# A two-stage graph network on one core: chunk residues in one row on VectorE, a residual moved on GpSimd, and the attention mask added by GpSimd instead of TensorE

## The reference

```python
h = relu(layernorm(x)); x = x + L0(h, adj)
h = relu(layernorm(x)); x = x + L1(h, adj)
# L0: scores = leaky_relu(f1[:, :, None] + f2[:, None, :], 0.2), -1e9 where adj == 0,
#     elu(softmax(scores) @ h)
# L1, for each of 3 layers l:
#     scores = leaky_relu(si[:, :, None] + sj[:, None, :] + attn_b[l], 0.2)
#     scores = where(adj + eye > 0, scores, -inf)
#     h = layernorm(x + softmax(scores) @ x, g1[l], beta1[l])
#     x = layernorm(h + gelu(h @ W1[l] + b1[l]) @ W2[l] + b2[l], g2[l], beta2[l])
```

## Time and profile before

| | |
|---|---|
| median of 3 runs | 2756.68 us (2756.49 to 2758.12) |
| profiled execution, its own time | 2756.0 us |
| its span, first to last instruction | 2754.2 us |
| TensorE clock granted, mean | 0.987 of full speed |
| busy: TensorE, VectorE, ScalarE, GpSimd | 96%, 78%, 80%, 61% |
| TensorE waits for a g_low before second / before hidden | 15.2 us in 29 waits / 5.6 us in 8 |

### The profile page before, as it was taken

How to read it: one execution, slowest core, us unless ns; L and a number is a source line. 1 busy time by engine, 2 the same in 40 slices (tenths; PEclk the granted TensorE clock), 3 DMA queues, 4 the chain that set the end, 5 groups by cost and what they waited for, 6 DMA issues and landing times.

```text
span 2754.2 us, 53331 instructions
## 1 busy us (share of the span) xinstructions
PE 2652.4 (96%) x16771; PEld 2388.7 (87%) x16868; DVE 2139.7 (78%) x7999; ACT 2201.9 (80%) x4494; POOL 1677.8 (61%) x2181
## 2 busy tenths in 40 slices
PE   4699999999999999999999999999999999999997
PEld 3688988898889898988898989898888898998997
DVE  6998787877787877787877888877888767677674
ACT  4889888888888888888887888888888777777774
POOL 4466666557676556566666566555676554454555
PEclk7899999999999999999999999999999999999999
DMA  6222222222122212122322121212132211111121
GB/s 203 75 73 85 70 94 73 77 74 94 63 93 66 77 64 74 51 76 81 100 74 88 45 81 66 78 56 89 60 104 81 68 36 52 42 46 53 50 64 54
DMA packets 118590, 203.43 MB, mean 74 GB/s; under 512 B 12801, under 2 KB 85537, under 8 KB 118305
## 3 DMA queue, kind: packets, MB, share of 16 engines
q1 hardware_dynamic: 118304, 199.97, 22.5%
HBM read 116.05 MB, written 83.89 MB: 73 GB/s over the span
## 4 chain that ended last, share of the span: by engine, by line
PE 72%; DVE 12%; POOL 8%; issue 5%; ACT 2%; DMA 1%; SPq 0%; DVEq 0%; POOLq 0%; ACTq 0%
PE bank L605 33%; PE bank L588 27%; PE ps_u L564 7%; POOL xo L374 3%; DVE g_lo L988 3%; DVE st L962 2%; POOL rs L1295 2%; PE ps_u L646 2%; PE ps_s L559 2%; DVE ub L1081 2%; PE ps_s L551 1%; POOL hb L374 1%; DVE ub L957 1%; ACT g_hi L862 1%; ACT bank L864 1%
## 5 line engine op out<-in xcount | busy, mean ns | idle before, releaser
L605 PE MATMUL bank<-w_hi,g_hi 128*128 128x256 f32 x3072 | 890.9, 290 | 15.4 <-DVE g_lo L988 15.2
L605 PE MATMUL bank<-w_hi,g_lo 128*128 128x256 f32 x3072 | 865.8, 282 | 0.0
L605 PE MATMUL bank<-w_lo,g_hi 128*128 128x256 f32 x3072 | 864.4, 281 | 0.0
L862 ACT ACTIVATE g_hi<-bank,b_eff 128x512 fp32r<-128x512 f32 x768 | 529.7, 690 | 334.2 <-PE bank L588 327.9
L988 DVE TENSOR_TENSOR g_lo<-bank,g_hi 128x512 fp32r<-128x512 f32 x768 | 519.5, 687 | 201.5 <-ACT bank L864 186.2
L588 PE MATMUL bank<-zt_hi,w_hi 128*128 128x512 f32 x1536 | 632.6, 412 | 9.3 <-DVE g_lo L988 5.6
L588 PE MATMUL bank<-zt_hi,w_lo 128*128 128x512 f32 x1536 | 607.4, 395 | 0.0
L588 PE MATMUL bank<-zt_lo,w_hi 128*128 128x512 f32 x1536 | 606.3, 395 | 0.0
L605 PEld LDWEIGHTS bank<-w_hi,g_hi 128*128 128x128 f32 x3072 | 579.5, 189 | 24.1 <-DVE g_lo L988 22.9
L605 PEld LDWEIGHTS bank<-w_lo,g_hi 128*128 128x128 f32 x3072 | 579.8, 189 | 0.8
L605 PEld LDWEIGHTS bank<-w_hi,g_lo 128*128 128x128 f32 x3072 | 579.2, 189 | 0.0
(11 more groups left out here) (96 smaller groups left out, 4141.1 us busy)
## 6 DMA issues: line engine op xcount, KB each, us to landing
xb<-x_scratch SPq DMA_DIRECT2D x88, 512.0 KB, 4.0
x_scratch<-xo SPq DMA_DIRECT2D x64, 512.0 KB, 4.8
xin<-in_x SPq DMA_DIRECT2D x38, 512.0 KB, 4.7
r_scratch<-elu_r SPq DMA_DIRECT2D x32, 512.0 KB, 3.0
xin<-r_scratch SPq DMA_DIRECT2D x32, 512.0 KB, 4.7
out<-xo SPq DMA_DIRECT2D x32, 512.0 KB, 3.6
m<-m_scratch SPq DMA_DIRECT2D x96, 128.0 KB, 3.7
x_scratch<-h SPq DMA_DIRECT2D x24, 512.0 KB, 2.9
```

Of the source, the lines that this page charges most:

```text
L605: mm = pe.matmul(y, g[:, c, r * P:(r + 1) * P], w[:, l, c, :], start=(c == 0 and n == 0), stop=(c == C - 1 and n == 2))
L862: act.activation(g_hi[:, c, :], block_in, ACT.Gelu, bias=bias).then_inc(g_hi_ready, 1)
```

## The change

Four edits. VectorE: `g_low(4)` to `g_low(7)` stand in one row, `second_statistics` behind them, with a small copy ahead of `second_variance`; in middle steps `first_lows` comes behind the first half of `next_dots`. GpSimd: `residual` of a unit moves from the end of step s+1 behind `first_root` of step s+2. ScalarE: in middle steps `second_norm` comes ahead of `first_exps`. And from step 5 on the mask is no longer added by TensorE in PSUM: GpSimd adds it to the relu tile that ScalarE makes (`e1` of unit s+2 at the start of step s, `e0` in middle steps), and `row_lows` waits for that (`masked_ready`) where it waited for `above_ready`. `spare` grows from 8 to 72 columns and its slices move.

```diff
+        def aside(u):
+            return u - 2 >= ASIDE
+        def aside0(v):
+            return early_step(v) + 1 >= ASIDE
...
                     if live(s + 1):
-                        sp.wait_ge(scores_ready, st.nth(s + 1))
+                        if aside(s + 1):
+                            sp.wait_ge(masked_ready, st.nth(s + 1 - 2 - ASIDE))
+                        else:
+                            sp.wait_ge(scores_ready, st.nth(s + 1))
...
-                pe.matmul(scores[:, :], ident_b[:, :], mask.rearrange("p t m -> p (t m)"),
-                          start=False, stop=True, skip_group_check=True).then_inc(done, 1)
+                if mask is not None:
+                    mm = pe.matmul(scores[:, :], ident_b[:, :], mask.rearrange("p t m -> p (t m)"),
+                                   start=False, stop=True, skip_group_check=True)
+                mm.then_inc(done, 1)
...
                 next_exps()
+                if only_middle(s) and not first_chunk:
+                    second_norm()
                 first_exps()
...
                 def next_lows():
                     if live(s + 2):
+                        taken = spare[:, 4 + T:5 + T]
+                        if aside(s + 2):
+                            row_lows(st.nth(s - ASIDE), taken, e1, ps_s, low, masked_ready, low_ready)
+                        else:
+                            row_lows(st.nth(s + 2), taken, e1, ps_s, low, above_ready, low_ready)
...
                 g_low(4)
                 g_low(5)
+                g_low(6)
+                g_low(7)
                 second_statistics()
-                g_low(6)
+                dve.tensor_copy(spare[:, 4:4 + T], neg_half[:, :])
                 second_variance()
-                g_low(7)
                 input_variance()
...
+                next_dots(range(T // 2))
                 if only_middle(s):
                     first_lows()
-                next_dots(range(T // 2))
...
+                def next_masked():
+                    if live(s + 2) and aside(s + 2):
+                        pool.wait_ge(above_ready, st.nth(s + 2))
+                        pool.wait_ge(m_in, 16 * st.nth(s + 2))
+                        take_waits(2)
+                        pool.tensor_tensor(e1[:, :, :], e1[:, :, :], m1[s % 2][:, :, :], ALU.add).then_inc(masked_ready, 1)
...
+                next_masked()
                 first_root()
                 if v3 is not None and v3 < CH:
                     made_root()
+                if live(s - 2) and s - 2 < U - 1:
+                    residual(pool, st, s - 2)
                 scaled_rows()
...
+                if only_middle(s):
+                    first_masked()
                 if v3 is not None and v3 >= CH:
                     made_root()
...
                     affine(pool, st, s - 1)
-                    residual(pool, st, s - 1)
```

More of the change, by code:

```diff
@@ L65, in build @@
     LATE = 4
+    ASIDE = 5
     U = L * G
@@ L225, in build @@
         above_ready = sem("above_ready")
+        masked_ready = sem("masked_ready")
         low_ready = sem("low_ready")
@@ L324, in early_norm @@
             return s == -1
+        def aside(u):
+            return u - 2 >= ASIDE
+        def aside0(v):
+            return early_step(v) + 1 >= ASIDE
+        ASIDE0 = min(v for v in range(G) if aside0(v))
         def x_rows(v):
@@ L884, in body @@
                     return
-                second_norm()
+                if not only_middle(s):
+                    second_norm()
                 make_rows()
@@ L1344, in made_root, with first_masked @@
                         inverse_root(st.nth0, v3, ve3, rs3, ve3_ready, rs3_ready)
+                def next_masked():
[4 more added lines that the diff above has]
+                        pool.tensor_tensor(e1[:, :, :], e1[:, :, :], m1[s % 2][:, :, :], ALU.add).then_inc(masked_ready, 1)
+                def first_masked():
+                    if v1 is not None and aside0(v1):
+                        pool.wait_ge(above0_ready, st.nth0(v1))
+                        pool.wait_ge(masks0_ready, st.nth0(v1))
+                        take_waits(3)
+                        pool.tensor_tensor(e0[:, :, :], e0[:, :, :], m0[:, :, :], ALU.add).then_inc(masked0_ready, 1)
                 def mask():
```

40 lines of the change are left out of this document (25 added, 15 removed).

## The result

The changed kernel takes 2784.61 us (median; 2784.34 to 2785.99) where the kernel before takes 2756.59: 1.0103 of its time (95% interval 1.009 to 1.0117), 28 us slower. The forecast was 2761.3 us, with a range of 2736 to 2778.

What follows compares the result with a forecast made beforehand. TensorE, busy 96%, was taken to bound the kernel: matmuls plus stops. Terms +29.9 - 20.8 - 3.0 - 5.1 - 4.4 + 2 + 6 = +4.6 us on 2756.0, median 0.7 above, gave 2761.3 us; range 2736 to 2778.

Steps and rivals of the forecast that it cites:

- middle steps 15 to 72: Twenty middle steps go from 546.1 to 576 us, as late VectorE work and GpSimd's mask add delay `hidden(7)`: +29.9 us.
- entering steps 14 to 71: Twenty entering steps lose the stop at g_low(7) and the mask's matmul, each falling to 26.03 us: -20.8 us.
- The residual: On GpSimd ahead of `scaled_rows`, it delays entering steps of layer 2 by 0.4 us in five steps: +2 us.
- steps 5, 8, 11: Early entering steps gain from the row of low halves and the mask's missing matmul: -3.0 us.
- late steps 7 to 73: In 23 late steps TensorE is not stopped and saves the mask's matmul of 0.22 us each: -5.1 us.
- steps 74 to 93: Twenty steps in which TensorE saves the mask's matmul of 0.22 us each: -4.4 us.
- steps 6, 9, 12: Early middle steps, already late from weight preparation, lose 1.9 us more each: +6 us.
- The row's part: In middle steps VectorE's `vb` starts 3.68 us in, not 2.00; without the add's wait the step takes 27.55 us.
- The add's part: GpSimd's mask add, taken as 1.35 us behind `affine`, makes row minima to g_low(3) 1.25 us later in middle steps.
- the two moves that were priced at nothing: ScalarE's `second_norm` ahead of `first_exps`, VectorE's `first_lows` behind half the dots, in middle steps: no cost, VectorE having over 0.5 us.
- The add is long: Rival: GpSimd's mask add takes 1.95 us, each middle step 0.6 us longer, +14 us, 2775 us; chance 0.20.
- The two faster cases: Rivals: add off the path, middle steps 27.55, 2732 us, chance 0.15; no lateness either, 26.44, 2705 us, chance 0.10.

Runs made afterwards that it cites:

- res_only: The kernel before with only the residual moved behind `first_root`, as the change moves it; 2766.17 us, ratio 1.0035.
- res_back: The changed kernel with the residual back behind `affine` at the end of GpSimd's step; 2800.72 us, ratio 1.016.
- g3_first: The changed kernel with g_low(3) ahead of `first_norm` in steps from 14 on that carry a residual; 2764.21 us, ratio 1.0022.
- row_only: The kernel before with only g_low(4) to g_low(7) in one row and the short copy ahead of `second_variance`; 2771.04 us, ratio 1.0054.
- mask_only: The kernel before with only the mask added by GpSimd to the relu tile from step 5 on; 2778.86 us, ratio 1.008.
- no_mid_add: The changed kernel with unit s+2's mask in middle steps up to 72 added by TensorE again; 2772.65 us, ratio 1.0055.
- no_swaps: The changed kernel with `second_norm` and the first dots of middle steps back in their old order; 2783.51 us, ratio 1.0098.
- part_only: The kernel before with g_low(6) ahead of `second_statistics`, g_low(7) inside it, and the short copy, in entering steps from 14 on; 2756.41 us, ratio 0.9999.

## Why the prediction was wrong

The direction was right, the size not: +28 us against +4.6. Term by term, from the steps of the two traces:

| term of the sum | forecast | measured |
|---|---|---|
| middle steps 15 to 72 | +29.9 | +32.5 |
| entering steps 14 to 71, with "The residual" | -20.8 + 2 | -14.7 |
| steps 5, 8, 11 | -3.0 | +0.9 |
| late steps 7 to 73 | -5.1 | +1.0 |
| steps 74 to 93 | -4.4 | +0.3 (to 95) |
| steps 6, 9, 12 | +6 | +6.1 |
| behind TensorE's last matmul | 0 | +2.4 |

**The step that failed is "The residual."** It was priced as later `scaled_rows` in five entering steps, "with VectorE's small instructions held on the way I take 0.4 us in five steps: +2", and nothing in late, plain and middle steps. What stood beside it was not a small instruction but `first_norm`, in every step that carries a residual: the group of 380 such instructions goes from 407 ns each to 506, in res_only to 507, in res_back back to 408. The rows with which it could have been seen were there: the earlier trace rows shows L973 held by just these four instructions, and `first_norm` waits for the very root behind which they were put. The prediction asked of L973 what a GpSimd instruction beside it does, and did not ask it of `first_norm`.

Against the forecast, in rounded means, this is 9 x 0.55 = 5.0 us in late steps, 6 x 0.8 = 4.8 in the last six and 3.7 in entering ones. In middle steps with a residual it is 9 x (29.63 - 28.8) = 7.5 more: the forecast had taken them to be as long as those without, and they are 1.3 longer. Together this is 21 us, and g3_first, which takes away only this way, is 20 us faster than the change. The move as such was no mistake beside the row and the mask, where it gains 16 us; its price was what the forecast had wrong.

**The middle steps** came out at 28.93 on the mean, against 28.8, but that is luck in part: those with a residual are 0.8 longer than forecast, those without 0.45 shorter. The row's part was right: `vb` at 3.59 (forecast 3.68), `affine`'s end at 9.26 (9.35), and 27.68 us with the row alone in row_only, where the sum without the add gives 28.8 - 1.25 = 27.55. The add's part was too large, 1.25 against 0.66. The add takes 1.17 us, not 1.35; the prediction's own rule, two instructions of 0.70 less a start-up of 0.20, gives 1.20, so the 1.35 does not follow from it. It also starts 9.34 into the step, not 9.60, so it ends at 10.53 and not 10.95, and `hidden(7)` starts 14.15 in, where 14.67 was forecast. That the row alone already lengthens the middle step, and the add only on top of it, is what the sum said, and row_only, mask_only and no_mid_add show it.

**The entering and late steps without a residual** (26.05, forecast 26.03; 28.22, forecast 28.21) and the plain ones were right. Late step 7 is an exception: it takes 29.10 us, and 28.22 in no_swaps, so there the two moves that were priced at nothing cost 0.9.

**Steps 5, 8 and 11** lose where they should gain: row_only has them at 26.26 us, mask_only at 28.42 (27.03 before), so it is the mask's add, for which the prediction had no price there. GpSimd in step 8, which begins at 340.42 in the kernel before and at 340.43 in mask_only, is busy with weight preparation and then `affine` until 8.8 us into the step in both. Then comes `first_root` in the one and the add in the other, so the root starts 1.3 us later:

```profile
349.18 1.02 POOL L1295 TENSOR_TENSOR rs<-ve,neg_half 128x4 f32<-128x4 f32 x1
```

```profile
349.34 1.18 POOL L1379 TENSOR_TENSOR e<-e,m 128x512 f32<-128x512 f32 x1
350.46 1.03 POOL L1323 TENSOR_TENSOR rs<-ve,neg_half 128x4 f32<-128x4 f32 x1
```

**The end** had no term in the sum: the program ends 15.1 us behind TensorE's last matmul before and 17.5 after. It is the row's doing, since row_only ends 17.6 behind and mask_only and res_only 15.1. In the last steps the row had no stop to take away, but it puts the statistics of unit 94 behind g_low(7) and all that follows them 2.2 us later. The last unit's root (the last row here) then finds GpSimd still at the unit before:

```profile
2761.08 2.83 POOL L387 TENSOR_TENSOR xo<-xo,g_row 128x256 f32<-128x256 f32 x4 [2.39 <-ACT xo L759]
2763.99 2.78 POOL L387 TENSOR_TENSOR xo<-xo,beta_row 128x256 f32<-128x256 f32 x4
2766.85 2.76 POOL L387 TENSOR_TENSOR xo<-xo,xin 128x256 f32<-128x256 f32 x4
2769.57 1.02 POOL L1327 TENSOR_TENSOR rs<-ve,neg_half 128x4 f32<-128x4 f32 x1
```

In part_only, which changes entering steps alone, the same root waits for its own variance only, and the span ends 2.4 us nearer to TensorE's last matmul:

```profile
2741.38 1.02 POOL L1338 TENSOR_TENSOR rs<-ve,neg_half 128x4 f32<-128x4 f32 x1 [0.64 <-DVE ve L997]
```

None of the rivals was this one. "The add is long" gave the nearest time (2775) for a reason that did not occur. The two faster cases needed middle steps of 27.55 us or less; they are 28.35 and 29.63.

## What to carry to other kernels

Work that is moved to just behind an instruction runs beside whatever else that instruction releases: before moving it, list who waits for the same semaphore on the other engines, and whether the two may run at the same time. An engine with a fixed order gains nothing from an earlier start of one piece if a wait in front of the next is thereby exposed; price a move in the step behind as well, and in the last steps of the program. And apply each part only in the kinds of step where the trace shows room: the change's edits cost 28 us when made everywhere; the useful ones, placed by kind of step and with two reorderings beside them, gave 30.

## What the runs showed of the hardware

VectorE's `first_norm` (tensor_scalar, 128x256, fp32, SBUF to SBUF) beside GpSimd instructions of the same size: its four instructions take 1.38 us alone, 1.62 beside four one-input instructions of 0.43, 2.74 beside four two-input ones of 0.75, and in these two cases the last ends 0.14 to 0.16 us behind GpSimd's last. GpSimd is hardly slowed (2.98 for four two-input ones, 2.81 alone). The Trainium skill, SBUF — State Buffer, section "Who interferes with whom", says that a tensor_scalar can enter a 2-port mode and that whoever issues first then gets the shared port pair for the whole instruction. The traces agree that GpSimd instructions of this size hold it, one-input ones too (1.62 us in place of 1.38); in which mode `first_norm` runs, no run here shows.

GpSimd's 128x512 addition (fp32 and bf16 in, fp32 out) takes 1.17 us, less than two 128x256 additions (0.75 each), and it holds even a 128x4 tensor_scalar of VectorE (L996 in step 54, 1.02 us in place of 0.17).
